# Masked MLP of a fused four-layer kernel: search steps taken out of the down-product slots and paced over the others

## The reference

```python
s = silu(x @ w_gate.T)                 # 1376 columns for each token
k = int(0.5 * 1376)                    # the 688 smallest |s| of each token ...
_, idx = top_k(-abs(s), k)
s = s.at[rows, idx].set(0.0)           # ... are set to zero, ties by index
return (s * (x @ w_up.T)) @ w_down.T
```

## Time and profile before

| | us |
|---|---|
| median of 3 runs | 2164.5 (2162.3 to 2167.2) |
| the profiled execution, device time | 2164.9 |
| its span in the trace | 2163.1 |
| TensorE matmuls busy | 2014.5 (93%) |
| VectorE busy | 1565.1 (72%) |
| ScalarE busy | 1020.2 (47%) |
| GpSimd busy | 560.5 (26%) |
| mean granted TensorE clock | 0.969 of full |

### The profile page before, as it was taken

How to read it: one execution, slowest core, us unless ns; L and a number is a source line. 1 busy time by engine, 2 the same in 40 slices (tenths; PEclk the granted TensorE clock), 3 DMA queues, 4 the chain that set the end, 5 groups by cost and what they waited for, 6 DMA issues and landing times. The chain is left out here.

```text
span 2163.1 us, 38405 instructions
## 1 busy us (share of the span) xinstructions
PE 2014.5 (93%) x14288; PEld 1236.3 (57%) x14288; DVE 1565.1 (72%) x2736; ACT 1020.2 (47%) x1658; POOL 560.5 (26%) x587
## 2 busy tenths in 40 slices
PE   5887999999999977899999999999999999999989
PEld 2342344444444344677667667666666666666756
DVE  6775677777777432169888988978889889788941
ACT  3221356565655621156366454553664545535511
POOL 2223453842523332111210311212103112121221
PEclk9997799999999988999999999999999999999999
DMA  7766235432333164020222013013130130131000
GB/s 258 234 214 176 70 95 137 126 86 68 93 95 83 33 196 167 9 98 1 87 72 100 6 53 120 6 53 119 59 125 1 54 115 1 53 115 53 11 11 11
DMA packets 115656, 187.35 MB, mean 87 GB/s; under 512 B 43200, under 2 KB 68176, under 8 KB 115520
## 3 DMA queue, kind: packets, MB, share of 16 engines
q1 hardware_dynamic: 91344, 133.22, 19.9%
q0 software_dynamic: 9088, 32.12, 5.3%
q10 hardware_dynamic: 15088, 20.19, 2.7%
HBM read 151.59 MB, written 33.62 MB: 86 GB/s over the span
## 5 line engine op out<-in xcount | busy, mean ns | idle before, releaser
L842 DVE TENSOR_REDUCE mx<-s 128x1 f32<-128x512 f32 (+3 forms) x608 | 380.9, 660 | 128.8 <-PE s L731 75.0
L823 ACT ACTIVATE pr<-s 128x1024 f32<-128x1024 f32 (+3 forms) x352 | 300.7, 868 | 243.8 <-PE s L750 181.7
L1467 ACT ACTIVATE kept<-ax,T 128x1376 f16<-128x1376 f32 x248 | 357.0, 1439 | 122.0 <-DVE T L1541 116.1
L1535 DVE TENSOR_SCALAR_CACHE_REDUCE junk<-ax,T 128x1376 f16<-128x1376 f32 x248 | 406.5, 1639 | 3.1 <-DVE T L1528 0.5
L1326 POOL TENSOR_TENSOR lohi<-h,lohi 128x256 f16<-128x256 f32 x224 | 173.6, 775 | 872.9 <-ACT lohi L1478 872.7
L1364 PE MATMUL ga<-xT_f,w_gate 128*128 128x256 f16 x2688 | 332.7, 274 | 7.9 <-DVE h L1592 4.9
L1374 PE MATMUL acc<-w_down,lohi 128*128 128x512 f16 x1344 | 326.3, 379 | 8.7 <-POOL lohi L1326 8.7
L1364 PE MATMUL ub<-xT_f,w_up 128*128 128x256 f16 x2688 | 331.6, 273 | 0.0
L1364 PEld LDWEIGHTS ga<-xT_f,w_gate 128*128 128x128 f16 x2688 | 263.3, 98 | 79.9 <-DVE h L1592 7.5
L1364 PEld LDWEIGHTS ub<-xT_f,w_up 128*128 128x128 f16 x2688 | 263.9, 98 | 31.2
L728 PE MATMUL s<-K,Q 65*128 65x512 f16 (+3 forms) x768 | 245.2, 345 | 26.3 <-DMA K<-onerow 13.5
(11 more groups left out here) (142 smaller groups left out, 2352.5 us busy)
## 6 DMA issues: line engine op xcount, KB each, us to landing
ring<-wgu_scr SPq DMA_DIRECT2D x64, 688.0 KB, 5.3
ring<-wd_scr SPq DMA_DIRECT2D x24, 768.0 KB, 4.7
wgu_scr<-tk_h POOLq DMA_DIRECT2D x16, 344.0 KB, 6.0
q_scr<-qk_h ACTq DMA_DIRECT2D x16, 256.0 KB, 4.0
k_scr<-qk_h ACTq DMA_DIRECT2D x16, 256.0 KB, 2.5
v_scr<-v_f ACTq DMA_DIRECT2D x16, 256.0 KB, 2.9
Q<-q_scr SPq DMA_DIRECT2D x32, 128.0 KB
K<-k_scr SPq DMA_DIRECT2D x32, 128.0 KB
```

The source lines that it names most:

```text
L823: nc.scalar.activation(pr[:, kb % 2, j0:j1, 0:w], scores, ACT.Exp, scale=SCALE).then_inc(e2_ok, 1)
L842: nc.vector.tensor_reduce(dst, s1[u % 2][:, 0:(j1 - j0) * w].rearrange("p (j k) -> p j k", k=w), AX.X, ALU.max).then_inc(r1_ok, 1)
L1467: nc.scalar.activation(kept[0][:, :], ax[k % 2][:, 1, :], ACT.Sign, scale=-1.0, bias=TF[:, 1:2], accum_out=cnt[:, 1:2]).then_inc(c1_ok, 1)
L1535: nc.vector.tensor_scalar(junk[:, :], ax[k % 2][:, 0, :], TF[:, 0:1], -float(KZERO), ALU.is_lt, ALU.add, accum_out=cnt[:, 0:1]).then_inc(c ...
```

## The change

Two things in the planner `mlp_stages`, nothing in what is computed and nothing in any engine's code:

1. No item may go into a slot of a down stage. Such a slot's span is also set equal to its own duty, so that it adds almost nothing to the budget.
2. The item costs are set to new values (a step 2380 ns in place of 2450, and small changes in the 18 finishing items).

```diff
     spans = {"f1": 3860, "f2": 3860, "gates": 3460, "down": 1800}
     evictions = {"f1": 430, "f2": 430, "gates": 530, "down": 460}
-    costs = [2450] * N_BITS + [80, 1740, 150, 950, 3180, 1650, 1900, 250, 250, 1740, 150, 150, 1740, 150, 950, 3180,
-                               1650, 1900]
+    costs = [2380] * N_BITS + [80, 1730, 150, 940, 3110, 1660, 1690, 250, 250, 1730, 150, 150, 1730, 150, 940, 3110,
+                               1660, 1690]
     first, last = at["gates", 0] + 1, at["down", NC - 1]
-    own = [(p, slot, spans[s.kind], evictions[s.kind] + 700 * len(slot.taken) + 1800 * len(slot.stats)
+    own = [(p, slot, spans[s.kind] if s.kind != "down" else evictions["down"] + 700 * len(slot.taken), evictions[s.kind] + 700 * len(slot.taken) + 1800 * len(slot.stats)
             + 1100 * len(slot.scaled) + 1400 * len(slot.lows))
            for p, s in enumerate(stages[first:last], first) for slot in s.slots]
...
         budget = min(budget + span * rate - duty, 6000)
-        while items and p > at["gates", items[0][0]]:
+        while items and p > at["gates", items[0][0]] and stages[p].kind != "down":
             k, item = items[0]
```

## The result

The changed kernel takes 2210.7 us (median of 6 runs, 2196.3 to 2215.9) against 2165.9 us (6 runs, 2162.3 to 2173.9) before: a ratio of 1.0187, 95% interval 1.0143 to 1.0231. The forecast was 2203 us, slower. A second set of runs of the same kernel gave 2208.3 us and 1.0166 (1.0130 to 1.0201).

What follows compares the result with a forecast made beforehand. The prediction took TensorE to set the pace with VectorE close behind, and VectorE to bind after the change. Its terms, 7.2 + 6.8 + 6.9 + 6.3 + 12.3 - 1.2 = +38 on 2164.9, gave 2203 us, range 2185 to 2216.

Steps and rivals of the forecast that it cites:

- cover: Rival: VectorE's gaps in f and gates stages take in the moved steps, only down waits change; 2149 us, chance 0.08.
- even: Rival: a still smaller cost than in Balance leaves the kernel at 2165 us; chance 0.03.
- Balance: Rival: waits are half of those summed ahead of the downs, the rest as forecast; total 2183 us, chance 0.10.
- the five terms: Added time in downs 0 to 1, 1 to 2, 3 to 4, 4 to 5 and stages 28 and 29: 39.5 us.
- four full stretches: Downs 0 to 1, 1 to 2, 3 to 4, 4 to 5, with VectorE full: +7.2, +6.8, +6.9, +6.3 us.
- Downs 0, 3, 6: Downs after a gates stage: waits of 2.54 and 0.20 us go, 1.62 stays; -2.7, -2.7, -3.6 us.
- The stretches ahead of them: Stages that end in downs 0, 3, 6: new waits of 2.7, 3.0, 2.1 us; with the downs -1.2 us.
- the walk: Slot-by-slot calculation ahead of downs 0, 3, 6, blocks waiting for TensorE or `inner`; it gave waits of 2.7, 3.0, 2.1 us.
- the +55: Upper bound on the total: each of the 34 moved steps also meets `low`, at 0.49 us each, 17 us more.
- the clock: Rival: waits at the start of downs 1, 2, 4, 5 make the clock fall; +6 to +10, 2212 us, chance 0.14.
- The fixed 21.7 us: From the last `inner` of an f stage through the down to the next f stage: 21.7 us, claimed to stay.
- Stages 28 and 29: Steps there go from 25 to 31 with no cover left, so the last mask comes +12.3 us later.

Runs made afterwards that it cites:

- experiment 4: The changed kernel with 25 search steps in place of 31 for each chunk; one run, 2166.9 us, MLP stretch 1236.7 us.
- experiment 3: The changed kernel with 56 unused matmuls put ahead of the last product of the f stage at downs 1, 2, 4, 5; ratio 1.0108 against before.
- experiment 2: Two runs, each one half of the change on the kernel before: new costs alone, ratio 1.0031; ban and short span with old costs, ratio 1.0113.

## Why the prediction was right, and where it was not

- **The bound.** That VectorE has no room for 34 more steps outside the downs held: waits of TensorE grew by 17.9 us in all, and with 25 steps in place of 31 the waits at the downs went (experiment 4). The rivals *cover* and *even* are out. *Balance* is out as a total (2183), but in its waits it was nearer than my forecast: it had the five terms at 20 in place of 39.5, all of it waits, and their waits grew by 25.3 (16.8 in the four full stretches, 8.5 in stages 28 to 30). I had given it 0.10. TensorE waits 1.5 us or more in 8 of the 14 f stages, where I had said most.
- **Downs 0, 3, 6.** Predicted -2.7, -2.7 and -3.6 (the last with its clock fall); measured -3.3, -3.3 and -4.4. The 2.54 and 0.20 went and the 1.62 stayed, as the earlier trace rows said; the rest is that downs are 0.6 us shorter beyond the waits.
- **The stretches ahead of them.** I put waits of 2.7, 3.0 and 2.1 us there; they are 0.2, 0 and 0.4. With the downs, -1.2 was forecast and -9.8 measured. The step that failed is the walk: it had VectorE full where it was not. In stages 14 and 15, ahead of down 3, VectorE is busy for 48.08 of 53.1 and 28.50 of 31.4 us and TensorE never waits. One term of it is the price of a step in an f slot. I charged the meeting of L1539 with `low`, 0.49 us, to each f slot that holds a step, 153 before and 156 after. The group of L1539 gives what the meetings cost. Before it is 107.3 us for 248 operations: less 248 x 0.23 that is 50.3. For the changed kernel:

```profile
L1539 DVE TENSOR_SCALAR pat<-cnt,pow 128x2 int32<-128x2 f32 x248 | 117.2, 472 | 9.2 <-ACT kept L1467 0.3
```

60.2 us. In the timelines 119 of the 248 operations take longer than 0.35 us before and 121 after, and all of them overlap a GpSimd operation. So the edit adds two meetings, as good as the 3 that I had, but both levels were some 35 too high: 156 x 0.49 is 76.4 us where 60.2 were paid, 16 us too much of VectorE's time spread over the phase. The meetings are also more complete: 27 of the 119 were partial ones, under 0.6 us, and 1 of the 121 is. A second term is L1557, for which I took its mean of 1.98. Its 2.72 us before are a meeting with the mask (beside L1331 at 1481.24), and ahead of down 3 this meeting is gone:

```profile
1517.26 0.16 DVE L1557 TENSOR_TENSOR step<-succ,T 128x1 f32<-128x1 f32 x1
```

With 8 and 7 meetings for the 12 and 10 slots with steps in stages 14 and 25, the two terms are 3.8 and 3.3 us too high ahead of downs 3 and 6. That is an estimate from these rows, and it is more than the waits of 3.0 and 2.1 that I had there; the walk was not done again with these prices. The lock of the Trainium skill ("SBUF — State Buffer", Who interferes with whom) says what a meeting costs, and the trace agrees in that 120 of the 121 take over 0.6 us; it does not say how many there are, and the +55, with a meeting for each of the 34 moved steps, is out.
- **The four full stretches.** Forecast +7.2, +6.8, +6.9, +6.3, together 27.2; measured +9.9, +8.3, +7.4, +8.4, together 34.1. But of these only 16.8 are waits. The rest, some 17, is the low clock in downs 1, 2, 4, 5 (11.6 by experiment 3) and behind the 2 us waits in the f stages. This was my rival *the clock*, with chance 0.14, at +6 to +10 on top. So what came was the forecast with waits smaller than I had them, and the clock rival beside it, larger. I had them as alternatives; they are one chain, since in the downs it is the wait that brings the clock down (experiment 3), though not each time (experiment 2). By its own sign, a granted clock in the downs under 0.95, the forecast is wrong in the clock: it is 0.88 and 0.82. The downs take 27.8 and 28.7 us where I had 25 to 27, which is what they take at the full clock (25.3 in experiments 2 and 3).
- **The fixed 21.7 us from the last `inner` of an f stage to the next f stage** are 24.2 at down 1 of the changed kernel (1259.05 to 1283.3). In the kernel with filled waits they are 1266.1 - 1244.4 = 21.7 again: the chain is as I said, and the clock made it longer.
- **Stages 28 and 29.** Forecast +12.3 at the last mask. The row:

```profile
2119.53 2.79 POOL L1331 TENSOR_TENSOR pp<-pp,kept 128x1376 f32<-128x1376 f32 x1 [1.53 <-DVE kept L1585]
```

117.8 us behind the start of stage 28, against 2070.37 - 1963.7 = 106.7 before: +11.1. With down 7 the stretch is +12.9. This term, which rested on a chain with no cover, came out nearest.
- **The total.** +38 was forecast and +37.4 measured in the MLP stretch, but as a sum of other terms. In waits alone the forecast was 39.5 + 7.8 - 2.7 - 2.7 - 2.5 = 39.4 us and the measurement 17.9; in clock it was -1.1 and 18.9. Sign, bound and places were right, and the closeness of the number is owed to two errors of some 20 us each that cancel. The first median lies 7.4 us further out and the second 3.6 us less far; for the two profiled executions the remaining 13.6 of the 51 us lie ahead of stage 1.
- **The planner's rate.** The loop itself gives 0.985 to 1.107 before, where I had 1.04 as its top (the peaks are in the gates stages), and 1.03 to 1.13 after. Nothing in the sum hangs on it.

## What to carry to other kernels

Where a slower engine is full, a place that looks harmful for its work may be the cheapest it has. Ask first how much of that place can stay (one step in a slot, none in the first) before all of it is given up: 19.0 and 18.5 us is the whole difference in downs 0, 3 and 6. And price a wait of TensorE at more than its length, since the clock that falls behind it can cost as much again (here 17.9 us of waits and 18.9 of clock). What meetings with another engine's operation cost is taken best from the mean of the operation's group, and how many there are from the timeline, not from the order of the code.

## What the runs showed of the hardware

- Waits of 5.4 us in pieces at the start of a down were followed by a clock of 0.88 and 0.82 over the stage in all four downs of both profiles of the changed kernel (27.8 to 28.8 us). With the ban and the old costs the same waits left the clock at 1.00 in downs 1 and 2 and not in downs 4 and 5. A wait of 2.07 us was followed by a fall in stage 6 and not in stage 17, and in stage 17 too in another profile. In each of four downs 56 small matmuls into an unused piece of a bank cost nothing and gave back 11.6 us over the four.
- A 128x2 VectorE operation of 0.23 us took 0.72 beside a GpSimd operation of 0.67, and a 128x1 one of 0.16 us took 2.72 beside one of 2.79.
- The phases ahead of stage 1 end between 905.8 and 921.7 us in eleven profiles of the same code, at a mean clock of 0.77 to 0.85 in one stretch of 200 us. A median over few runs of this program therefore can hardly tell 5 us apart; the stretch that the change touches repeats to 0.2 us in two profiles of one kernel.
